# Four transposes of a normed row block: in a row behind head 12, or singly behind heads 13 and 14

## What is computed

```python
x = _layernorm(x + _L0_attn_ref(x, Wq, Wk, Wv, Wo))     # attention ends in: out @ Wo.T
x = _layernorm(x + _L0_ffn_ref(x, ...))                 # begins with: fwht(x * SU_ug) / SCALE
```

## Time and profile before

| | |
|---|---|
| time, median of 3 runs | 2310.42 us |
| all runs | 2312.11, 2310.42, 2307.86 us |
| span of the profiled execution, first to last instruction | 2310.1 us |
| PE busy | 2254.4 us (98%) |
| DVE busy | 1825.1 us (79%) |
| ACT busy | 1273.1 us (55%) |
| POOL busy | 1129.0 us (49%) |
| mean granted clock of TensorE | 0.994 of full speed |
| heads of the second stage (L478) | 3 x 512 matmuls, 202.9, 200.4 and 200.3 us busy |
| transposes (L449) | 128, 20.4 us busy in the second stage |

### The profile page before, as it was taken

How to read it: one execution, slowest core, us unless ns; L and a number is a source line. 1 busy time by engine, 2 the same in 40 slices (tenths; PEclk the granted TensorE clock), 3 DMA queues, 4 the chain that set the end, 5 groups by cost and what they waited for, 6 DMA issues and landing times.

```text
span 2310.1 us, 32819 instructions
## 1 busy us (share of the span) xinstructions
PE 2254.4 (98%) x10209; PEld 1823.0 (79%) x10209; DVE 1825.1 (79%) x2452; ACT 1273.1 (55%) x2285; POOL 1129.0 (49%) x1002
## 2 busy tenths in 40 slices
PE   7999999999999999999999989999999999999998
PEld 5778787787878786787777768888888888888887
DVE  7877777778686868787887896787888788878877
ACT  6666666666676767233334455454545554455443
POOL 4667676767676767455544733321242133303321
PEclk9999999999999999999999999999999999999999
DMA  4110101111120215777767541323233323222323
GB/s 153 37 65 37 68 34 66 47 58 62 39 73 28 73 60 192 255 246 254 245 229 261 187 140 62 123 78 113 79 101 92 118 81 98 92 82 83 98 67 101
DMA packets 132701, 252.75 MB, mean 109 GB/s; under 512 B 44576, under 2 KB 45344, under 8 KB 122880
## 3 DMA queue, kind: packets, MB, share of 16 engines
q1 hardware_dynamic: 132608, 251.60, 32.5%
HBM read 188.11 MB, written 63.44 MB: 109 GB/s over the span
## 4 chain that ended last, share of the span: by engine, by line
PE 71%; issue 11%; POOL 9%; DVE 5%; ACT 2%; DMA 1%; SPq 0%; POOLq 0%; ACTq 0%; DVEq 0%
PE pj L548 17%; PE pj L629 11%; PE pnum L629 6%; PE pj L643 5%; PE psc L629 5%; PE pj L558 4%; PE pst L629 4%; PE psc L643 4%; PE pnum L643 3%; PE psc L579 3%; PE pnum L597 3%; PE pnum L600 3%; PE pst L643 2%; POOL fa L1338 2%; PE pst L586 1%
## 5 line engine op out<-in xcount | busy, mean ns | idle before, releaser
L1368 POOL TENSOR_TENSOR wcs<-wcr 128x256 f32<-128x256 f32 x64 | 67.7, 1058 | 515.3 <-DVE wcl L1107 504.3
L1401 POOL TENSOR_TENSOR tb<-tb,sinb 128x512 f32<-128x512 f32 x160 | 224.0, 1400 | 91.7 <-ACT tb L928 90.9
L548 PE MATMUL pj<-xah,wqh 128*128 128x512 f32 x512 | 204.3, 399 | 4.3 <-DVE Kf L1243 3.0
L1404 POOL TENSOR_TENSOR Ql<-tb,Qh 128x512 fp32r<-128x512 f32 x128 | 169.7, 1328 | 70.2 <-ACT Qh L937 70.1
L478 PE MATMUL pj<-woh,oh 128*128 128x512 f32 x512 | 202.9, 396 | 0.0
L548 PE MATMUL pj<-xal,wqh 128*128 128x512 f32 x512 | 200.5, 392 | 0.0
L548 PE MATMUL pj<-xah,wql 128*128 128x512 f32 x512 | 200.5, 392 | 0.0
L478 PE MATMUL pj<-woh,ol 128*128 128x512 f32 x512 | 200.4, 391 | 0.0
L478 PE MATMUL pj<-wol,oh 128*128 128x512 f32 x512 | 200.3, 391 | 0.0
L1231 DVE TENSOR_TENSOR pj<-pj,cosb 128x512 f32<-128x512 f32 x160 | 111.1, 694 | 69.7 <-ACT tb L928 69.6
L629 PE MATMUL pj<-xch,wch 128*128 128x512 f32 x384 | 150.9, 393 | 7.9 <-DVE xcl L1113 4.7
(11 more groups left out here) (258 smaller groups left out, 7070.8 us busy)
## 6 DMA issues: line engine op xcount, KB each, us to landing
num_scratch<-no SPq DMA_DIRECT2D x128, 256.0 KB, 2.4
nt<-num_scratch SPq DMA_DIRECT2D x32, 1024.0 KB, 5.5
rb<-rden_scratch SPq DMA_DIRECT2D x32, 1024.0 KB, 6.3
wdr<-wd_scratch SPq DMA_DIRECT2D x128, 256.0 KB, 3.3
wcr<-in_wg SPq DMA_DIRECT2D x64, 256.0 KB, 2.8
wcr<-in_wu SPq DMA_DIRECT2D x64, 256.0 KB, 3.1
xst<-in_xT SPq DMA_DIRECT2D x34, 256.0 KB, 3.8
xr<-in_x SPq DMA_DIRECT2D x32, 256.0 KB, 5.6
```

The source lines that it names most:

```text
L548: last = nc.tensor.matmul(bank[:, :], w[:, b, :], x[:, b, :], start=(k == 0), stop=(k == 11))
L1401: nc.gpsimd.tensor_tensor(tb[c][:, :], tb[c][:, :], sinb[:, :], ALU.mult).then_inc(sin_done, 1)
L1404: nc.gpsimd.tensor_tensor(Ql[g % 2][:, c, :], (tb[c] if c else Kf)[:, :], f32(Qh[g % 2][:, c, :]), ALU.subtract).then_inc(lo_done, 1)
```

## The change

The four transposes, their waits and their semaphore stay as they are. Their places among the matmuls of the heads differ: the first comes behind the last matmul of head 13, the others behind the first, the second and the third of head 14. With j = 1 the fold of the weights, which stays behind head 12, thereby comes before them; with j = 3 the last transpose is directly ahead of the transform.

```diff
+ROW_TRANSPOSES = ((13, 2), (14, 0), (14, 1), (14, 2))
...
             def transposes(s, n, at):
-                pe.wait_ge(x1_ready, n + 1)
-                if at >= 2:
-                    pe.wait_ge(tr_free, n - 1)
                 for c in range(DC):
-                    last = nc.tensor.transpose(pt[s][:, c, :], x1[s][:, c * P:(c + 1) * P], identb[:, :])
-                last.then_inc(tr_done, 1)
+                    row_transpose(s, n, at, c)
+
+            def row_transpose(s, n, at, c):
+                if c == 0:
+                    pe.wait_ge(x1_ready, n + 1)
+                    if at >= 2:
+                        pe.wait_ge(tr_free, n - 1)
+                last = nc.tensor.transpose(pt[s][:, c, :], x1[s][:, c * P:(c + 1) * P], identb[:, :])
+                if c == DC - 1:
+                    last.then_inc(tr_done, 1)
...
-            def head(s, h, at):
+            def head(s, h, at, n):
...
                     last = nc.tensor.matmul(py[s][:, :], a[s][:, h, :], b[:, h, :], start=(h == 0 and i == 0),
                                             stop=(h == H - 1 and i == 2))
+                    if at >= 1 and (h, i) in ROW_TRANSPOSES:
+                        row_transpose(1 - s, n - 1, at - 1, ROW_TRANSPOSES.index((h, i)))
...
-                    last = head(s, h, at)
-                    if h == 12 and at >= 1:
-                        transposes(1 - s, n - 1, at - 1)
+                    last = head(s, h, at, n)
                     if h == 12 and j == 1 and at >= NCH:
                         fold(m - 1)
```

More of the change, by code:

```diff
@@ L487, in between @@
                     for h in range(0, H // 4):
-                        head(0, h, 0)
+                        head(0, h, 0, 0)
             def step(m, j, at):
```

## The result

| | before | after |
|---|---|---|
| median of 7 runs each | 2310.42 us | 2316.78 us |
| lowest to highest | 2307.86 to 2312.42 | 2314.72 to 2319.55 |
| span of the profiled execution | 2310.1 us | 2316.0 us |

The ratio is 1.0026, with a 95% interval from 1.0015 to 1.0037: slower by 6.0 us, between 3.5 and 8.5. The prediction was 2315.3 us, 4.9 us more than before, in a range from 2310 to 2320.

What follows compares the result with a forecast made beforehand. The prediction took a closed ring through DVE, PE, ACT and POOL, not PE's own work, to bound the 50.00 us tile. Seven delays of 0.7 us, 4.9 us, gave 2315.3 us, range 2310 to 2320.

Steps and rivals of the forecast that it cites:

- The bound: Second stage: PE, busy 49.07 of 50.00 us a tile, waits because a closed ring of engines is longer.
- a ring through ACT, DVE and POOL: Closed chain DVE, PE's transposes, ACT, DVE, PE's transform, ACT, DVE, POOL, DVE; its length is the tile's 50.00 us.
- A lone transpose: One transpose between two matmuls of 512 columns costs PE 0.11 us; bounds nothing to 0.27 us.
- The last transpose with j = 2: Placed singly, the four last 1.34 us instead of 0.66, so ACT's copies begin 0.7 us later.
- The tile: One tile of the second stage takes 50.7 us in place of 50.00.
- Step 3: Front of the second stage, where the ring begins: last transpose also 0.7 us later, counted once.
- The other steps: Transposes with j = 3, 0 and 1: delays fall into gaps or existing waits and hold up nothing.
- The sum: Six tiles and step 3, seven times 0.7 us, give 4.9 us: 2315.3 us.
- Rival C: Step 2: shorter wait of 2.4 us keeps PE's clock up, ring starts 1.6 us earlier, 2313.7 us; chance 0.07.
- Rival A: PE sets the pace, so waits with j = 1 and 2 vanish: 7.8 us faster, 2302.6 us; chance 0.09.
- Rival B: The delay is taken up by closer copies or POOL's queue: no change, 2310.4 us; chance 0.11.
- Rival D: PE's clock falls at the transform in each tile, 1.6 us more each: 2324.9 us; chance 0.05.

Runs made afterwards that it cites:

- the late row: Kernel before, with the four transposes kept in a row but behind head 13 instead of head 12: ratio 1.0002, 2310.88 us.
- the run with only j = 2 restored: Changed kernel, but in steps with j = 2 the four transposes stand in a row behind head 12 as before: ratio 1.0001, 2311.53 us.
- only the two orders: Kernel before, ACT's sixteen folded-weight copies moved to j = 3, DVE's second butterflies ahead of divide: 2307.22 us; same on changed kernel: 2306.77 us.
- the cut rings: Kernel before with ACT's folded-weights high part moved ahead of its j = 3 copies, 2302.52 us; with copies and butterflies reordered, 2307.22; with all three, 2298.45.
- both rings cut: Changed kernel plus ACT's high part and sixteen copies moved into the j = 3 gap and DVE's second butterflies earlier: ratio 0.9946, 2297.07 us.

## Why the prediction was right, point by point

- **The bound.** Shown: PE, busy for 98%, was waiting on a ring through ACT, DVE and POOL. The ring could be cut at two joins without touching PE's work, and each time the tile took the length of the next ring: 48.83 for 48.9 expected, 49.40 for 49.4, 48.2 for 48.3.
- **A lone transpose**, 0.11 us from the last of a row: 0.115 to 0.12. The prediction's other estimate, 0.056 us, is the gap of an isolated matmul in the Trainium skill, "TensorE: Matmul & The Clock Gate", section "Back-to-back issue gap"; the same section says that this figure is too low where each matmul has a weight load, as here, and gives 0.081 us for a stream of them. The measurement decides: here a lone transpose among matmuls of 512 columns costs more than either, and twice the first.
- **The last transpose with j = 2**, 0.7 us later: 1.36 us from first start to last end for 0.66. PE waited 0.44 us at the new place (0.28 idle and 0.16 hidden), where 0.45 was worked out.
- **The tile**, 50.7 us: 50.74. From the end of the norm with j = 2 of tile 1 to the end of that of tile 7 it is 304.80 us for 300.32 before, 4.48 more for the six, where six times 0.7 is 4.2. The rest is that the distances above each grew by 0.01 or 0.02 us; why was not tried.
- **Step 3**, 0.7 us: from the norm in step 2 to that in step 6 the changed kernel takes 47.36 us, the one with the late row 46.65, both at full clock there, so that it costs 0.71.
- **The other steps** cost nothing in the steady tiles, as the run with only j = 2 restored shows (50.03 us a tile).
- **The sum.** Tiles and step 3 give 5.2 us, where seven times 0.7 was 4.9; the medians differ by more, 6.0 by the ratio, with an interval that holds both. The two profiled spans differ by 5.9, and not by these alone. The changed kernel's norm in step 2 ended 2.06 us later, and 1.87 of that was there at the first norm, before any edit could act; its clock then stayed up, which gave back 1.7; and after the second stage it lost 0.4. That 5.2 + 2.06 - 1.7 + 0.4 comes to 6.0 is the bookkeeping of two executions; what the traces show of the change is the 5.2.
- **Rival C** (the clock stays up in step 2) came about in the profiled execution: the wait in step 2 is 2.54 us for 3.05, and matmuls behind it stay 0.227 us apart, at 2.4 GHz. PE's timeline of the changed kernel, and its window (0.99 is the share of DMA):

```profile
963.97 0.33 PE L454 MATMUL psc<-identb,x 128*128 128x128 f32 x1 [2.54 <-DVE x L1011]
```

```profile
964.00:967.00 3.00, 3.00 (x16) 2.47 (x16) 2.97 (x3) 1.63 (x5) 0.00 (x0) 1.00 0.99 317
```

  Its price, forecast at 1.6 us, is 1.7: 48.37 us from the norm in step 2 to that in step 6 in the kernel before, 46.65 with the late row at full clock. But the change alone doesn't decide it. Seven of the thirteen profiled executions have the transposes of step 2 at the later place: behind waits of 2.37 to 2.39 us the clock fell in four of them, and behind 2.41, 2.42 and 2.54 us it stayed up in three. In the six with the old place it fell in five, behind waits of 3.04 to 3.09 us, and stayed up in one, that of only the two orders, behind 3.08. So either level can follow in both; whether the later place makes the higher one likelier, and how much of it is in the medians, isn't shown.
- **Rival A** (PE sets the pace) fell with the late row and with the cut rings. **Rival B** (the delay is taken up): no slack was found in the ring, 0.70 us went in and 0.75 came out. **Rival D** (the clock falls in each tile): the waits that it needs came, 0.70 us ahead of the transposes with j = 3 and 0.84 ahead of the transform, but the granted clock of the tile is 1.00.
- **What was near.** The bound for telling it from no change, 2315.0, lay in the middle of the forecast; that the result is above it owes something to luck.

PE's waits between 957 and 1335 us show the trade at a glance:

```profile
PE psc L454 <- DVE x L1011: 9.6, 15, 2.5
PE pj L465 <- DVE xsl L1034: 5.8, 7, 0.8
```

Placed behind three and more matmuls, the transposes wait for their norm for 9.6 us where it was 8.5, and the transform for 5.8 where it was 0.9.

## What to carry to other kernels

An engine that is busy for 98% need not set the pace: follow what its waits wait for until you come back to where you began, and if the sum of that ring is the period, only what lies in the ring counts, until another ring is the longer one. Work that feeds a waiting engine is worth ending early as a whole; spreading it between other work saved PE nothing here (0.115 to 0.12 us a transpose, 0.11 in a row) and delayed its last piece, and the last piece is what raises the semaphore. When a ring is found, look for work in it that could be done in a gap of the same engine (here ACT's high part and its sixteen copies): that gave 12 us where the placement of the transposes had nothing to give.

## What the runs showed of the hardware

- Up to the first norm the kernels have the same instructions, and yet its end lies between 942.2 and 946.8 us over the thirteen profiled executions. TensorE's clock at the start goes with a part of it: its mean over the first 100 us was 0.97 in the three executions with the earliest first norms and 0.93 in the ten others. Those ten still lie up to 3.4 us apart; why wasn't tried. Below are the changed kernel's window and that of the late row, 4.6 us apart at the first norm.

```profile
0.00:100.00 100.00, 81.24 (x331) 62.81 (x331) 75.34 (x107) 63.20 (x113) 50.14 (x50) 0.93 0.28 99
```

```profile
0.00:100.00 100.00, 79.13 (x332) 60.81 (x333) 75.78 (x107) 63.71 (x114) 50.56 (x51) 0.97 0.28 99
```

- A wait of PE in step 2 of 2.38 us was followed by 1.2 GHz in one execution and one of 2.42 us by 2.4 GHz in another, and so were waits of 3.05 and 3.08 us. A comparison of two profiled spans carries 1.7 us of that; the length of the tiles doesn't.
- Where the ring bounds them the steady tiles mostly repeat to a few hundredths of a us within an execution (tiles 1 to 5: 49.99 to 50.02 before, 50.74 or 50.75 after), a far finer measure than the time's scatter, 2306.4 to 2313.9 us over all executions of the kernel before. In the changed kernel with both rings cut they differ by up to 0.4 us (47.84 to 48.24).
